# Transformer block on eight cores: first stage reordered with late projections as fillers, and three edits in the experts

## The chip, the cores and the metric

The kernel runs on the 8 cores of one Trainium2 chip. Every core computes one batch element of 2048 rows with the same program and exchanges nothing with the others. The metric is the device time of the slowest core in microseconds (us). Its matmul engine is called PE below, the vector engine DVE, the scalar engine ACT, GpSimd POOL; SP is the engine whose queue issues plain DMAs.

## The reference

For each batch element (2048 rows of 1024) a parallel block is computed: row normalisation, then causal attention with 16 heads of 64, and beside it a mixture of 4 experts, of which each row uses 2.

```python
xn = _layernorm(x, axis=-1)
x = x + _L0_attn_ref(xn, w_qkv, w_out) + _L0_ffn_ref(xn, w1, b1, w2, b2, wr, br)

# _L0_attn_ref: q, k, v of xn; softmax(q k^T / 8, causal) v; then w_out
# _L0_ffn_ref:
logits = xf @ wr + br
topk_vals, topk_idx = jax.lax.top_k(logits, K)            # K = 2 of E = 4
gates = jax.nn.softmax(topk_vals, axis=-1)
h = jax.nn.gelu(jnp.einsum('nd,edh->enh', xf, w1) + b1[:, None, :], approximate=False)
y = jnp.einsum('enh,ehd->end', h, w2) + b2[:, None, :]
c = jnp.einsum('eh,ehd->ed', jax.nn.gelu(b1, approximate=False), w2) + b2
c_sum = c.sum(axis=0)
out = jnp.einsum('nk,nkd->nd', gates, y_sel - c_sel + c_sum[None, None, :])
```

The constants c of the four experts give every row an additional sum: a "constant row" that depends on its gates alone. The hidden size is 4096.

## The kernel before

Work is emitted engine by engine in program order. `W(engine, semaphore, value)` (L234) makes an engine wait, `I` (L238) emits an instruction that raises a semaphore, `E` (L246) one that does not. Each engine and each DMA-issuing queue runs its list in order.

**First stage (L254 to L529).** SP loads the rows of x in eight blocks of 256 rows (`xt`, L255), with the biases b1, the router weights wr (one partition, 16 KB) and br between the first and second block. PE then spreads wr to all partitions in eight pieces (L336) and ACT copies them out (L339). A loop over j (L503) handles two tiles of 128 rows each time: `norm_stats(j)` (DVE L442 to L453, ACT L455 and L457, POOL L461), `transpose_out` of the tiles of the turn before (DVE L497 for the even tile, ACT L499 for the odd), `norm_rows` (ACT L469 writes the normalised rows `xnb`, of which there are four buffers, and SP stores them to `xn_tm`, L475, one store waiting for the one before), V projections (`v_group`, 8 matmuls, evicted by ACT in this stage), Q and K projections of head pair 0 (`qk_group`, evicted by DVE L389), `transpose_in` (PE L483), and some halves of the router's logits (`logit`, DVE L428). From the fifth tile on, `norm_rows` waits for the store that last used its buffer: `W("scalar", "SXN", 16 * (ts - 3))`.

**Attention (L532 to L1037).** A head pair takes 40 steps (query tile qt of 512, key tile kb of 128): two score matmuls (L568), an exponential on ACT (L585), a causal mask on DVE (L591), two matmuls with V (L607). At the last kb of a qt DVE copies the result (L621). Between them `fill` pops single matmuls from a list of groups of 8, `pair_fill` (L941), spread over the pair by the planner's `cost` (L951). Pair hp holds the 8 Q/K groups of pair hp+1, and for hp below 4 also four V groups of heads 8 to 15. Without V groups a pair has 64 filler matmuls, with them 96. `load_wqk(hp + 2)` (L270) is issued by POOL at the start of a pair. `dveq` hands out the rest of the logits and the routing to DVE.

**Experts (L1049 to L1379).** An expert has two steps, u = 0 and 1, each over half of the hidden size. `emit_h` (L1085) makes 16 chunks hc of h (L1101, ACT GELU L1112), `emit_y` (L1244) multiplies tile by tile with w2 (32 matmuls, L1281), DVE scales into `yacc` (L1297, L1300), and in step u = 1 POOL adds each tile to y by an indirect DMA (`scatter`, L1065). Weights come by POOL's queue, four loads of w1 (L914) and four of w2 (L922) for each step. Steps are numbered 0 to 7. Depending on how many rows an expert gets on a core, a step has nine tiles (one of 64 rows) or eight. Two extra jobs run inside. The constants: `g_rows` (L1134) multiplies GELU(b1) with w2; for the last expert its w2 is loaded in eight pieces to `gw` by `load_gw` (L1205), the first at the start of `emit_y` of step 0, and read at tile 4 and at the last tile of steps 0 to 3. The constant rows: `dense` (L1223) makes one tile of 128 rows in PE (L1231), DVE copies it to one of four buffers (L1236) after the DMA that used that buffer has landed (`SCD`), and POOL adds it to y (L1241). All 16 run in step 6: eight in `emit_h`, after each odd hc, eight in `emit_y`, one before each of the tiles 0 to 7.

## Time and profile before

| | us |
|---|---|
| median of 3 runs | 1701.55 |
| lowest and highest run | 1693.19, 1892.82 |
| the profiled execution | 1698.15 |
| its slowest core, first to last instruction (the span) | 1696.6 |
| spans of the other seven cores | 1675.2 to 1692.7 |
| PE busy on the slowest core | 1508.3 (89%) |
| ACT, DVE, POOL busy | 637.6, 486.7, 215.2 |

All rows are of core 7, the slowest, unless they name another. The span begins with the first instruction of the core; 1.55 us of the profiled execution lie around it. A bracket at the end of a row of the timeline holds how long the engine had been idle and what ended it. "PEclk" is the share of the full TensorE clock that was granted.

### The profile page before, as it was taken

The page shows a single profiled execution, that of the slowest core. Times are in us where ns is not written, and L with a number is a line of the kernel's source. Part 1 is how long each engine was busy: PE and PEld are TensorE (multiplying, and loading weights), DVE is VectorE, ACT ScalarE, POOL GpSimd, SP SyncE. Part 2 cuts the span into 40 slices and gives each one's busy share as a digit, 9 for nine tenths or more (in the row PEclk, how much of TensorE's full clock was granted, in tenths as well). Part 3 has the DMA queues.
Part 4 walks back from the last instruction along what each step waited for, and adds up shares of the span by engine and source line. Part 5 has one row for each costly group of instructions (what it writes and reads, how often), then busy time and mean ns, then how long its engine had stood idle before and what let it go on. Part 6 is the DMA issues. An engine that isn't in the chain of part 4 may idle for free.

```text
span 1696.6 us, 22095 instructions; the slowest of 8 cores (1675.2 to 1696.6 us)
## 1 busy us (share of the span) xinstructions
PE 1508.3 (89%) x7616; PEld 664.6 (39%) x7616; DVE 486.7 (29%) x879; ACT 637.6 (38%) x809; POOL 215.2 (13%) x233
## 2 busy tenths in 40 slices
PE   4778889877888889989997999998999999978996
PEld 2333223222322235534643444443434445534642
DVE  3675665677333321122022012011011022122011
ACT  3448788766789762300400310400401402300410
POOL 2001211000001000102013002112020022111012
PEclk9989999988999799989999999999999999999998
DMA  8140000030004667685978934997942987894424
GB/s 249 63 75 1 13 14 1 13 50 14 13 15 99 137 139 176 155 127 114 153 120 133 142 50 88 170 140 107 143 93 34 141 132 114 126 143 76 87 40 75
DMA packets 113627, 160.14 MB, mean 94 GB/s; under 512 B 41813, under 2 KB 74709, under 8 KB 113113
## 3 DMA queue, kind: packets, MB, share of 16 engines
q0 software_dynamic: 66096, 119.55, 45.7%
q1 hardware_dynamic: 47402, 38.91, 8.8%
q8 instruction: 77, 1.26, 0.3%
q14 instruction: 52, 0.43, 0.1%
HBM read 194.09 MB, written 38.80 MB: 137 GB/s over the span
## 4 chain that ended last, share of the span: by engine, by line
PE 74%; ACT 7%; DVE 6%; DMA 6%; issue 5%; DVEq 1%; ACTq 0%; POOL 0%; SPq 0%; POOLq 0%; another core or an unknown queue 0%
PE P L1101 27%; PE P L1281 24%; PE P L382 5%; PE P L607 5%; ACT p L585 4%; PE P L568 4%; DMA y<-dst 2%; PE P L1179 2%; DMA gw<-w 2%; PE P L398 2%; DVE usb L621 2%; PE P L892 1%; PE P L1162 1%; ACT rcp L629 1%; ACT rcp L628 1%
## 5 line engine op out<-in xcount | busy, mean ns | idle before, releaser
L1101 PE MATMUL P<-xg,w1b 128*128 128x363 bf16 (+2 forms) x2560 | 468.8, 345 | 18.2 <-issue 15.7
L1281 PE MATMUL P<-w2b,h_sb 128*128 128x512 bf16 (+1 forms) x2176 | 467.4, 383 | 17.7 <-DVE yacc L1297 9.8
L1112 ACT ACTIVATE h_sb<-P,b_sb 128x363 bf16<-128x363 f32 (+1 forms) x320 | 195.2, 613 | 587.5 <-PE P L1101 505.6
L585 ACT ACTIVATE p<-P,cneg,c 128x1024 bf16<-128x1024 f32 (+1 forms) x320 | 330.0, 1072 | 76.4 <-PE P L568 67.3
L1101 PEld LDWEIGHTS P<-xg,w1b 128*128 128x128 bf16 x2560 | 251.3, 98 | 236.4 <-issue 31.1
L1281 PEld LDWEIGHTS P<-w2b,h_sb 128*128 128x128 bf16 (+1 forms) x2176 | 207.1, 99 | 279.0 <-issue 42.7
L607 PE MATMUL P<-p,v_sb 128*128 128x512 bf16 (+3 forms) x640 | 180.2, 362 | 20.4 <-DVE p L591 13.1
L382 PE MATMUL P<-xn_fm,wp 128*128 128x512 bf16 x512 | 150.1, 393 | 12.8 <-ACT v_sb L409 6.3
L568 PE MATMUL P<-q,k 64*128 64x512 bf16 (+3 forms) x640 | 119.1, 368 | 44.6 <-ACT p L585 43.8
L1300 DVE SCALAR_TENSOR_TENSOR yacc<-P,gate_sb,yacc 128x1024 f32<-128x1024 f32 x32 | 41.1, 1284 | 407.1 <-PE P L1281 401.5
L1297 DVE TENSOR_SCALAR yacc<-P,gate_sb 128x1024 f32<-128x1024 f32 x32 | 41.1, 1284 | 329.8 <-PE P L1281 323.3
L428 DVE SCALAR_TENSOR_TENSOR junk<-xt,mv,wr_bc 128x512 bf16<-128x512 f32 x128 | 101.6, 812 | 5.5
L568 PEld LDWEIGHTS P<-q,k 64*128 64x128 bf16 x640 | 32.5, 93 | 168.1 <-issue 167.1
L607 PEld LDWEIGHTS P<-p,v_sb 128*128 128x128 bf16 x640 | 57.4, 99 | 94.8 <-issue 48.3
L1112 ACT ACT_TABLE_LOAD x4 | 5.1, 1283 | 214.2 <-PE P L1101 214.2
L1081 POOL DMA_INDIRECT y<-yacc,idx_sb x32 | 50.4, 1576 | 248.6 <-DVE yacc L1300 167.0
L398 PE MATMUL P<-wv,xn_fm 128*128 128x512 bf16 x256 | 71.6, 406 | 1.6 <-DVE xn_fm L497 1.6
L914 POOL DMA_DIRECT2D w1b<-w x32 | 28.6, 922 | 344.3 <-PE P L1101 266.6
L382 PEld LDWEIGHTS P<-xn_fm,wp 128*128 128x128 bf16 x512 | 41.4, 98 | 77.1 <-issue 53.2
L591 DVE TENSOR_TENSOR p<-p,tri_bf 128x256 bf16<-128x256 bf16 x128 | 38.2, 303 | 98.6 <-ACT p L585 97.6
L639 POOL TENSOR_TENSOR cat<-usb,rcp 64x512 bf16<-64x512 f32 x24 | 32.5, 1352 | 106.9 <-ACT rcp L631 106.0
L621 DVE COPY usb<-P 128x512 f32<-128x512 f32 x64 | 41.2, 685 | 16.6 <-PE P L607 16.3
(163 smaller groups left out, 694.2 us busy)
## 6 DMA issues: line engine op xcount, KB each, us to landing
w1b<-w POOLq DMA_DIRECT2D x32, 1024.0 KB, 16.1
w2b<-w POOLq DMA_DIRECT2D x32, 1024.0 KB, 18.4
xt<-x SPq DMA_DIRECT2D x8, 1024.0 KB, 19.0
xr<-x SPq DMA_DIRECT2D x16, 512.0 KB, 4.3
y<-xr SPq DMA_DIRECT2D x16, 512.0 KB, 5.0
gw<-w POOLq DMA_DIRECT2D x8, 1024.0 KB
y<-dst POOLq DMA_DIRECT2D x16, 512.0 KB, 11.2
wp<-wqk POOLq DMA_DIRECT2D x8, 512.0 KB, 6.0
```

The lines of the kernel that those rows point to most:

```text
L382: mms = [lambda t, bank, dc=dc: t.matmul(bank, w[:, dc * 256 + o:dc * 256 + o + 128], xn_fm[:, dc * S + tt * 512:dc * S + (tt + 1) * 512], ...
L398: mms = [lambda t, bank, dc=dc: t.matmul(bank, xn_fm[:, dc * S + ts * 128:dc * S + (ts + 1) * 128], wv[half][:, dc * 512:(dc + 1) * 512], ...
L428: E("vector", lambda v: v.scalar_tensor_tensor(junk[:, half * 512:(half + 1) * 512], xtile(ts)[:, half * 512:(half + 1) * 512], mv[:, 2 * ...
L568: fn = (lambda t, h=h: t.matmul(sb[:, h * 512:h * 512 + n], k_sb[hp % 2][h * 64:h * 64 + 64, kb * 128:(kb + 1) * 128], q_sb[hp % 2][h * 64 ...
L585: v_exp[i] = I("scalar", "SS", lambda s: s.activation(dst, src, AF.Exp, bias=cneg8[:, 0:1], scale=c0125[:, 0:1]))
L607: fn = (lambda t, h=h: t.matmul(P45[:, h * 512 + qo:(h + 1) * 512], v_sb[:, o + h * 64:o + h * 64 + 128], p[:, h * 512:h * 512 + n], start ...
L621: last_u[h] = ("SV", I("vector", "SV", lambda v, h=h: v.tensor_copy(u[:, h * 512:(h + 1) * 512], P45[:, h * 512:(h + 1) * 512])))
L1081: I("gpsimd", "SA%d" % (t % 2), lambda g: g.indirect_dma_start(y_h.ap(), bass.IndirectOffsetOnAxis(idx_sb[:, q:q + 1], 0), yacc[:, t * 102 ...
L1101: fn = (lambda t, b=b, hc=hc, dc=dc, o=o, n=n, bank=bank: t.matmul(bank[:, 0:n], w1b[b][:, dc * 512 + (hc % 4) * 128:dc * 512 + (hc % 4 + ...
L1112: geluv[i] = I("scalar", "SS", lambda s, hc=hc, o=o, n=n, bank=bank, col=col: s.activation(h_sb[:, hc * PITCH + o:hc * PITCH + o + n], ban ...
L1281: fn = (lambda tt, b=b, k=k, off=off, rows=rows, r=r, half=half, pt=pt: tt.matmul(pt[r:r + rows, half * 512:(half + 1) * 512], h_sb[:, k * ...
L1297: evict[i] = I("vector", "SV", lambda v, t=t, gate=gate, pt=pt: v.tensor_scalar_mul(yacc[:, t * 1024:(t + 1) * 1024], pt[:], gate))
```

## The change

It has these parts:

- The router weights come as one DMA that writes all 128 partitions (2 MB), last of SP's first loads; the spreading by PE and ACT goes. The eight loads of x stand back to back. The bias columns and GELU(b1) are made later (end of the first stage, start of the experts).
- In the loop of the first stage the statistics of block j+1 come ahead of the logits and the projections of turn j. The loop has nine turns; logits begin in turn 3 with 6, then 7, 7, 7, 7, 6. The V groups of tiles 12 to 15 and the Q/K groups of query tiles 2 and 3 of pair 0 leave it.
- Those eight groups become fillers of pair 0 (16 groups, 128 matmuls). The V groups of the other heads move to pairs 1, 2 and 3 (5, 5 and 6 instead of 4 in each of pairs 0 to 3). The load of wqk for pair 2 comes at qt = 3 of pair 0. A fourth place for `usb` is used in the first half of pair 0, since the old one still holds V weights.
- In the experts, the first `load_gw` is issued after chunk 13 of `emit_h` of step 0, behind the last w2 load of that step and ahead of the last waits for step 1's w1.
- `dense` runs three times in `emit_h` of step 6 (chunks 5, 9, 13), eight times in `emit_y` of step 6, and five times in `emit_h` of step 7.
- The last tile of step 7 is computed in two halves of 512 columns; each is scaled and added to y by a DMA of its own.

```diff
@@ -182,7 +183,7 @@
     p_sb = [at(f"p{i}", [128, 1024], BF16, o_p + 2048 * i) for i in range(3)]
     rcp = at("rcp", [128, 512], F32, o_p + 6144)
 
-    usb = [at(f"usb{i}", [128, 1024], F32, o) for i, o in enumerate((o_wv, o_p + 16384, o_qk))]
+    usb = [at(f"usb{i}", [128, 1024], F32, o) for i, o in enumerate((o_wv, o_p + 16384, o_qk, o_qk + 12288))]
     coefT = at("coefT", [128, S], BF16, o_p + 20480)
     cat = at("cat", [128, NPAIR * S], BF16, o_cat)
     wv = [at(f"wv{i}", [128, 4096], BF16, o_wv + 8192 * i) for i in range(2)]
@@ -255,14 +256,13 @@
         I("sync", f"SXD{j}", lambda e, j=j: e.dma_start(
             xt[2 * j][:].rearrange("p (t d) -> p t d", d=1024),
             x_h.ap()[j * 256:(j + 1) * 256, :].rearrange("(t p) d -> p t d", p=128)), 16)
-        if j == 0:
-            v_b1 = I("sync", "SX", lambda e: e.dma_start(
-                b1st[:].rearrange("r (k c) -> r k c", k=4),
-                b1_h.ap().rearrange("k (r c) -> r k c", r=32)), 16)
-            v_wr = I("sync", "SX", lambda e: e.dma_start(
-                wr_bc[0:1, :], wr_h.ap().rearrange("(a k) d -> a (k d)", a=1)), 16)
-            v_br = I("sync", "SWR", lambda e: e.dma_start(
-                br_bc[:], bass.AP(br_h, 0, [[0, 128], [1, 4]])), 16)
+    v_b1 = I("sync", "SX", lambda e: e.dma_start(
+        b1st[:].rearrange("r (k c) -> r k c", k=4),
+        b1_h.ap().rearrange("k (r c) -> r k c", r=32)), 16)
+    v_br = I("sync", "SWR", lambda e: e.dma_start(
+        br_bc[:], bass.AP(br_h, 0, [[0, 128], [1, 4]])), 16)
+    v_wr = I("sync", "SWRB", lambda e: e.dma_start(
+        wr_bc[:], bass.AP(wr_h, 0, [[0, 128], [1, 4096]])), 16)
 
     v_wq = {}
 
@@ -317,31 +317,17 @@
 
     W("scalar", "SG", v_c1)
     W("tensor", "SG", v_c1)
-    W("tensor", "SX", v_b1)
...
-    W("tensor", "SX", v_wr)
-    v_wb = {}
-    for c in range(8):
-        bank = (P45, P67)[c // 2 % 2][:, c % 2 * 512:(c % 2 + 1) * 512]
-        if c == 0:
-            W("tensor", "SS", v_b1c)
-        if c >= 4:
-            W("tensor", "SS", v_wb[c - 4])
-        v_t = I("tensor", "ST", lambda t, c=c, bank=bank: t.matmul(
-            bank, onesq[0:1, :], wr_bc[0:1, c * 512:(c + 1) * 512], start=True, stop=True))
+
+    def bias_columns():
+        W("tensor", "SX", v_b1)
+        v_t = 0
+        for e_ in range(NE):
+            v_t = I("tensor", "ST", lambda t, e_=e_: t.transpose(
+                P45[0:128, e_ * 32:(e_ + 1) * 32], b1st[0:32, e_ * 128:(e_ + 1) * 128], ident[0:32, 0:32]))
         W("scalar", "ST", v_t)
-        v_wb[c] = I("scalar", "SS", lambda s, c=c, bank=bank: s.activation(
-            wr_bc[:, c * 512:(c + 1) * 512], bank, AF.Identity))
-    W("scalar", "SS", v_b1c)
-    v_hf = I("scalar", "SS", lambda s: s.activation(hfake[:], b1_sb[:], AF.Gelu))
-
-    guard = [("SS", v_wb[6]), ("SS", v_wb[7])]
+        return I("scalar", "SS", lambda s: s.activation(b1_sb[:], P45[:, 0:128], AF.Identity))
+
+    guard = [("SS", 0), ("SS", 0)]
     bank_i = [0]
     trg = [("ST", 0), ("ST", 0)]
     xn_ev = {}
@@ -386,6 +372,8 @@
 
         def evict(bank, v):
             W("vector", "ST", v)
+            if hp == 1 and tt == 0:
+                W("vector", *u_read[0])
             e = I("vector", "SV", lambda d: d.tensor_copy(dst[:, tt * 512:(tt + 1) * 512], bank))
             (q_ev if isq else k_ev)[(hp, tt)] = ("SV", e)
             return ("SV", e)
@@ -500,10 +488,9 @@
         trg[ts % 2] = xn_ev[ts]
 
     first_logits = [(ts, k, half) for ts in (0, 1, 2, 3, 8) for k in range(NE) for half in range(2)]
-    for j in range(10):
-        if j < 8:
-            v_nm = norm_stats(j)
-        if 1 <= j <= 8:
+    v_nm = norm_stats(0)
+    for j in range(9):
+        if j >= 1:
             transpose_out(2 * j - 2)
             transpose_out(2 * j - 1)
         if j < 8:
@@ -511,29 +498,33 @@
             norm_rows(2 * j + 1, v_nm)
             if j == 6:
                 load_wqk(1)
-        if j >= 2:
+        if j < 7:
+            v_nm = norm_stats(j + 1)
+        for _ in range((0, 0, 0, 6, 7, 7, 7, 7, 6)[j]):
+            logit(*first_logits.pop(0))
+        if 2 <= j < 8:
             for ts in (2 * j - 4, 2 * j - 3):
                 run_all(v_group(0, ts, True))
-            if j % 2 == 1:
+            if j % 2 == 1 and j < 7:
                 run_all(qk_group(0, (j - 3) // 2, False))
                 run_all(qk_group(0, (j - 3) // 2, True))
         if j < 8:
             transpose_in(2 * j)
             transpose_in(2 * j + 1)
-        for _ in range((0, 0, 4, 5, 5, 5, 5, 5, 5, 6)[j]):
-            logit(*first_logits.pop(0))
         if j == 5:
             E("vector", lambda v: v.drain())
             v_t01 = I("vector", "SV", lambda v: v.memset(cnt[:, 0:1], 0.0))
             W("gpsimd", "SV", v_t01)
             load_wv(1)
 
+    v_b1c = bias_columns()
+
 
     steps = [(hp, qt, kb) for hp in range(NPAIR) for qt in range(4) for kb in range(4 * qt + 4)]
     n_st = len(steps)
     v_qk, v_exp, v_msk, v_av = {}, {}, {}, {}
     v_mult = {}
-    last_u = [("SV", C["SV"])] * 2
+    last_u = [("SS", v_b1c)] * 2
     u_read = [("SG", C["SG"])]
     pend, later = [], []
     W("scalar", "SV", C["SV"])
@@ -943,9 +940,15 @@
         a = []
         for tt in range(4):
             a += [qk_group(hp + 1, tt, False), qk_group(hp + 1, tt, True)]
-        if hp < 4:
-            vs = [v_group(1, ts, False) for ts in range(4 * hp, 4 * hp + 4)]
-            a = [x for pr in zip(a[0::2], a[1::2], vs) for x in pr]
+        if 1 <= hp <= 3:
+            vs = [v_group(1, ts, False) for ts in ((), range(0, 5), range(5, 10), range(10, 16))[hp]]
+            a = [x for q in range(4) for x in a[2 * q:2 * q + 2] + vs[q:q + 1]] + vs[4:]
+        if hp == 0:
+            late = []
+            for ts in range(12, 16):
+                late.append(v_group(0, ts, False))
+            a = [qk_group(0, 2, False), qk_group(0, 2, True)] + late + \
+                [qk_group(0, 3, False), qk_group(0, 3, True)] + a
         pair_fill[hp] = [(x, 8) for x in a]
 
     def cost(i):
@@ -967,12 +970,13 @@
             tot = sum(u for _, u in pair_fill[hp])
             cum, csum_ = 0.0, sum(cost(k) for k in range(i, i + 40))
             popped[0] = 0
-            if hp < NPAIR - 2:
-
-                W("gpsimd", "ST", C["ST"])
-                load_wqk(hp + 2)
             if hp == NPAIR - 1:
                 W("gpsimd", "ST", C["ST"])
+        if hp < NPAIR - 2 and kb == 0 and qt == (0 if hp else 3):
+
+            assert ("k", hp, 3) in done and ("q", hp, 3) in done
+            W("gpsimd", "ST", C["ST"])
+            load_wqk(hp + 2)
         if hp == 4 and qt == 0 and kb == 3:
             W("gpsimd", "ST", C["ST"])
             W("gpsimd", *u_read[0])
@@ -1039,6 +1043,8 @@
         W("tensor", *g_)
 
 
+    DENSE = [(6, hc) for hc in (5, 9, 13)] + [(7, hc) for hc in (1, 4, 7, 10, 13)]
+
     PH = [P45[:, 0:512], P45[:, 512:1024], P67[:, 0:512], P67[:, 512:1024]]
     PY = [P01, P23]
 
@@ -1084,6 +1090,8 @@
 
         def emit_h(step, cols):
             e_, u = divmod(step, 2)
+            if first and step == 0:
+                E("scalar", lambda s: s.activation(hfake[:], b1_sb[:], AF.Gelu))
             if u == 0:
                 W("tensor", "SXT", xgv[e_])
             for hc in range(16):
@@ -1115,7 +1123,7 @@
                     gel[(step, hc)] = geluv[i]
                 if hc % 4 == 3:
                     hblk[(step, b)] = v_g
-                if first and step == 6 and hc % 2 and state["ts"] < NTS:
+                if first and (step, hc) in DENSE:
                     dense()
                 if first and step == 0 and o_late:
                     o_tile(o_late.pop(0))
@@ -1123,6 +1131,8 @@
                     W("gpsimd", "ST", v_g)
                     W("gpsimd", *u_read[0])
                     emit_w2(0, hc // 4)
+                    if hc == 13:
+                        load_gw()
 
         def py_next():
             i = state["y"]
...
@@ -1241,13 +1251,37 @@
             I("gpsimd", f"SCD{ts % 4}", lambda g: g.dma_start(
                 y_h.ap()[ts * 128:(ts + 1) * 128, :], dst4[ts % 4][:], accum_op=ALU.add), 16)
 
+        def last_tile(t):
+
+            i, pt = py_next()
+            q = tile_q(NE - 1, t)
+            for half in range(2):
+                c = slice(half * 512, (half + 1) * 512)
+                v_y = 0
+                for hc in range(16):
+                    fn = (lambda tt, hc=hc, c=c: tt.matmul(
+                        pt[:, c], h_sb[:, hc * PITCH + t * 128:hc * PITCH + t * 128 + 128],
+                        w2b[hc // 4][:, (hc % 4) * 1024 + c.start:(hc % 4) * 1024 + c.stop],
+                        start=(hc == 0), stop=(hc == 15)))
+                    if hc == 15:
+                        v_y = I("tensor", "ST", fn)
+                    else:
+                        E("tensor", fn)
+                W("vector", "ST", v_y)
+                yc = yacc[:, t * 1024 + half * 512:t * 1024 + (half + 1) * 512]
+                evict[i] = I("vector", "SV", lambda v, c=c, yc=yc: v.scalar_tensor_tensor(
+                    yc, pt[:, c], gate_sb[:, q:q + 1], yc, ALU.mult, ALU.add))
+                W("gpsimd", "SV", evict[i])
+                I("gpsimd", f"SAL{half}", lambda g, half=half, yc=yc: g.indirect_dma_start(
+                    y_h.ap().rearrange("s (h c) -> (s h) c", h=2),
+                    bass.IndirectOffsetOnAxis(idx2[:, half:half + 1], 0), yc, None, compute_op=ALU.add), 16)
+
         def emit_y(step, tiles):
             e_, u = divmod(step, 2)
             v_ga = 0
             last = len(tiles) - 1
             if first and step == 0:
                 c_init()
-                load_gw()
             for p, (off, rows) in enumerate(tiles):
                 t = off // 128
                 if first and step < 6 and p == 1:
@@ -1262,8 +1296,11 @@
                     load_gw()
                 if first and step < 6 and p == 2:
                     g_sum(e_, v_ga)
-                if first and step == 6 and state["ts"] < NTS:
+                if first and step == 6 and p < 8:
                     dense()
+                if first and step == 7 and p == last:
+                    last_tile(t)
+                    break
                 i, pt = py_next()
                 v_y = 0
                 for hc in range(16):
```

## Rows read from the trace of the kernel before

**Rows 1.** Cores, the slowest: span and mean granted clock
```profile
core 7: 1696.6 us, clock 0.961
```

**Rows 2.** Chain of work that ended last, in order of time: start us, us, what
```profile
15.54 14.00 PE P L336 x16
```

**Rows 3.** L255 at 18 to 19 us, the last load of x: duration ns, start; landing
```profile
L255 SPq DMA_DIRECT2D xt<-x x1: 3027/3027/3027, 18.4 to 18.4; - x1
DMA to landing us min/median/max: 21.6/21.6/21.6
```

**Rows 4.** L475 at 34 to 34.5 us, the first store of normalised rows
```profile
L475 SPq DMA_DIRECT2D xn_tm<-xnb x1: 345/345/345, 34.2 to 34.2; - x1
DMA to landing us min/median/max: 6.5/6.5/6.5
```

**Rows 5.** Page, DMA issues: out<-in, engine, count, KB each, median us to landing
```profile
xn_tm<-xnb SPq DMA_DIRECT2D x16, 256.0 KB, 2.2
```

**Rows 6.** Windows: span, length, PE, PEld, DVE, ACT, POOL busy, PEclk, DMA share, GB/s
```profile
24.00:27.00 3.00, 3.00 (x5) 1.23 (x4) 1.15 (x5) 1.19 (x2) 0.00 (x0) 1.00 1.00 328
```

**Rows 7.** Timeline of DVE, a turn of the first stage: start us, us, what
```profile
55.84 0.69 DVE L389 CAST q<-P 128x512 bf16<-128x512 f32 x1 [1.04 <-PE P L382]
56.62 0.75 DVE L428 SCALAR_TENSOR_TENSOR junk<-xt,mv,wr_bc 128x512 bf16<-128x512 f32 x1
...
60.32 2.47 DVE L442 BATCH_NORM_STATS2 bst<-xt 128x6 f32<-128x512 f32 x4
...
63.34 1.23 DVE L497 CAST xn_fm<-P 128x1024 bf16<-128x1024 f32 x1
```

**Rows 8.** Timeline of ACT: rows 4 and 5 normalised, and the first exponential
```profile
42.08 2.36 ACT L469 ACTIVATE xnb<-xt,nmr_a,r_a 128x1024 bf16<-128x1024 f32 x2
...
117.94 2.75 ACT L585 ACTIVATE p<-P,cneg,c 128x1024 bf16<-128x1024 f32 x3 [3.76 <-DVE q L389]
```

**Rows 9.** Timeline of DVE: the copy at the end of pairs 1, 2, 5 and 6
```profile
240.15 1.28 DVE L621 COPY usb<-P 128x512 f32<-128x512 f32 x2
...
300.76 1.28 DVE L621 COPY usb<-P 128x512 f32<-128x512 f32 x2
...
501.24 1.28 DVE L621 COPY usb<-P 128x512 f32<-128x512 f32 x2
...
555.49 1.28 DVE L621 COPY usb<-P 128x512 f32<-128x512 f32 x2
```

**Rows 10.** Timeline of PE: tile 4 of step 0, and of step 1
```profile
757.01 1.04 PE L1140 MATMUL P<-gw,hfake 128*32 128x512 bf16 x8 [8.06 <-DMA gw<-w]
757.98 26.18 PE L1281 MATMUL P<-w2b,h_sb 128*64 128x512 bf16 x128
...
886.50 0.61 PE L1140 MATMUL P<-gw,hfake 128*32 128x512 bf16 x8
888.11 24.47 PE L1281 MATMUL P<-w2b,h_sb 128*64 128x512 bf16 x128 [0.99 <-DVE yacc L1300]
```

**Rows 11.** Timeline of POOL: DMA issues at the ends of h of steps 0 and 6
```profile
718.92 0.77 POOL L1211 DMA_DIRECT2D gw<-w  x1
...
1481.83 3.84 POOL L914 DMA_DIRECT2D w1b<-w  x4
```

**Rows 12.** Timeline of PE in step 6, emit_y: tile 0, constant row ahead of tile 5, tile 5
```profile
1480.98 7.07 PE L1281 MATMUL P<-w2b,h_sb 128*128 128x512 bf16 x32 [1.33 <-DVE dst L1236]
...
1529.05 1.01 PE L1231 MATMUL P<-cst,coefT 96*128 96x512 bf16 x2 [9.86 <-DVE dst L1236]
1530.13 8.42 PE L1281 MATMUL P<-w2b,h_sb 128*128 128x512 bf16 x32
```

**Rows 13.** Chain of work that ended last, in order of time
```profile
1485.36 42.12 DMA y<-dst
...
1680.91 1.29 DVE yacc L1300
```

**Rows 14.** Windows at the end of the span, same columns as rows 6
```profile
1686.00:1688.00 2.00, 0.00 (x0) 0.00 (x0) 0.00 (x0) 0.00 (x0) 0.00 (x0) 0.50 0.98 186
```

More of the change, by code:

```diff
@@ L156, in build_nc @@
     gateh = small("gateh", [128, 4])
+    idx2 = small("idx2", [128, 2], I32)
     unf = small("unf", [128, 64])
@@ L422, in logit @@
         if (ts, k, half) == (0, 0, 0):
-            W("vector", "SS", v_wb[7])
+            W("vector", "SWRB", v_wr)
             W("vector", "SWR", C["SWR"])
@@ L616, in emit_av @@
         if sp:
-            u = usb[0 if hp < 4 else 1 if hp < NPAIR - 1 else 2]
+            u = usb[3 if hp == 0 and qt < 2 else 0 if hp < 4 else 1 if hp < NPAIR - 1 else 2]
             W("vector", "ST", v_av[i])
@@ L838, in evict @@
                 gate_sb[:, e_ * 16:(e_ + 1) * 16], cmpa[:, 96:112], cmpa[:, 64:80], ALU.add))
+            if e_ == NE - 1:
+                for half in range(2):
+                    VD(lambda d, half=half: d.tensor_scalar(
+                        cmpa[:, 112 + half:113 + half], cmpa[:, 87:88], 2.0, float(half), ALU.mult, ALU.add))
+                E("vector", lambda d: d.tensor_copy(idx2[:], cmpa[:, 112:114]))
             for r in (0, 64):
@@ L1242, in dense @@
                 y_h.ap()[ts * 128:(ts + 1) * 128, :], dst4[ts % 4][:], accum_op=ALU.add), 16)
+        def last_tile(t):
+            i, pt = py_next()
+            q = tile_q(NE - 1, t)
+            for half in range(2):
+                c = slice(half * 512, (half + 1) * 512)
[17 more added lines that the diff above has]
+                    bass.IndirectOffsetOnAxis(idx2[:, half:half + 1], 0), yc, None, compute_op=ALU.add), 16)
         def emit_y(step, tiles):
@@ L1375, in ffn @@
                 expert(e_, *EVEN)
-        W("gpsimd", "SA0", C["SA0"])
-        W("gpsimd", "SA1", C["SA1"])
+        for k in ("SA0", "SA1", "SAL0", "SAL1"):
+            W("gpsimd", k, C[k])
     ffn(0, PITCH // 128, True)
```

10 lines of the change are left out of this document (2 added, 8 removed).

## Prediction, made before the changed kernel was run

> **What bounds the kernel now.** I read the page first: PE is busy 89% of the span, so time can be won only where PE stands still, runs at half clock, or at the end. The view of the cores gives the time that counts, core 7 with 1696.6 us [rows 1]; the profiled execution took 1698.15 us, 1.55 us around the span. Then I followed the chain of waits and the timelines stage by stage.
>
> *First stage, to 117.94 us.* PE spends 14 us spreading the router weights [rows 2], and ACT, which copies them out, normalises nothing meanwhile. But that is not all that holds the stage. The last block of x is issued at 18.4 us and lands 21.6 us later, at 40.0 [rows 3]. The first store of normalised rows, issued at 34.2, lands at 40.7 [rows 4], 6.5 us later where the usual store takes 2.2 [rows 5]: SP's transfers land in their order. The fifth tile, which needs that store's buffer, is normalised at 42.08 [rows 8]. After that the stage is a ring: DVE computes five logits in 60.32 - 56.62 = 3.70 us and only then the statistics of the next block, 3.02 us [rows 7]; ACT waits for these, PE for ACT, and DVE for PE's projections. The first exponential starts at 117.94 [rows 8].
>
> *Attention.* Pair 6, with 64 fillers, takes 555.49 - 501.24 = 54.25 us from the end of pair 5 to its own; pair 2, with 96, takes 300.76 - 240.15 = 60.61 [rows 9]. A filler costs (60.61 - 54.25)/32 = 0.20 us: PE is nearly the bound, and there is little idle time for more.
>
> *Experts.* PE runs almost without a gap. One gap is the first wait for `gw` [rows 10], another the constant row before tile 5 of step 6, which waits for a DMA of 42.12 us [rows 12, 13].
>
> **The change part by part.**
>
> *Opening.* PE's 14 us and ACT's copies go. This alone doesn't start the fifth tile earlier: its buffer still waits for the first store, and that store now stands behind x and behind 2 MB of router weights. Loads ran at 328 GB/s with the DMA engines full [rows 6]: 2 MB take 6.4 us. The x blocks end at 40.0 as before (the engines are full from early on, with x and POOL's weights; the order of x changes, not the sum), the router weights at 46.4, the store 0.7 later, at 47.1. The fifth tile starts 5.0 us later than before, not earlier.
>
> The Trainium skill (DMA: Bandwidth & Descriptors, Bandwidth) times one load of 1 MB at 6.15 us, which would make 12.3 us of the 2 MB and 1680 of the sum below; the trace, with loads in a queue, has 6.4 in rows 6.
>
> *The turns.* From the fifth tile to the end of the next evicted q took 55.84 + 0.69 - 42.08 = 14.4 us before [rows 7, 8]. The opening turn 3 has the same members, so 61.5. From there the statistics are early, PE and ACT have less than DVE, and DVE sets the pace. A turn costs it 1.2 (copy) + 3.0 (statistics) + 7 x 0.74 = 9.4 us. Turns 4, 5 and 6: 28.2, with two evictions of 0.69 in turn 5 29.6; turn 7 without statistics 6.4; the copy in turn 8 1.2. Sum 37.2, so 98.7; with the first scores (estimated at 0.8 with their hand-overs) the first exponential starts at 99.5. That is 18.4 us earlier. Six logits still stand on DVE before the first mask, as before, so that costs nothing new. The bias columns (four small transposes, one copy) lie on PE and ACT in those turns, where both wait for DVE; without that cover about 1 us. GELU(b1) moves to ACT ahead of its first chunk, where PE is the slower; nothing.
>
> *The fillers.* Eight groups of 8 matmuls leave the stage, 64 fillers come into attention (32 more in pair 0; 8, 8 and 16 in pairs 1 to 3). At 0.20 each +12.7 us. Lower bound 8, if a third falls into waits for exponentials; upper 64 x 7.07/32 = 14.1, the full price of a matmul [rows 12]. Their eight evictions (0.69 each) go to DVE in pair 0, which has room while PE is the bound. The load of wqk for pair 2 goes one whole query tile ahead of its use: nothing. POOL waits there for PE's latest matmul; behind it stand only normalisations of `cat`, needed in the last pair.
>
> *gw.* With the wait, tile 4 of step 0 costs 8.06 + 1.04 + 26.18 = 35.3 us; the same stretch in step 1, 0.61 + 0.99 + 24.47 = 26.1 [rows 10]. The difference, 9.2, includes matmuls at the lower clock behind the gap. `gw` was issued at 718.92, behind four w1 loads [rows 11]. Now it is issued just behind the last w2 load, some 7 us earlier and with 4 MB fewer ahead; it lands well before 749. The w1 loads that it overtakes land when `gw` did before (757 at the latest) and are needed only at the next step, near 785. -9.2. Bound: -7, if something else is late there.
>
> *Constant rows.* The number of matmuls is the same. At the border of h and y two constant rows no longer collide: -1.3 [rows 12]. The gap before tile 5: 9.86, less the ordinary 0.99, plus 0.40 and 1.35 for slow matmuls behind it [rows 10, 12], 10.6 us. What was late is the DMA of the constant row of tile 0, queued behind four w1 loads that began at 1481.83 [rows 11], landing 45.7 us after them [rows 13]. The row that waits now still uses a buffer four rows back, and that is again tile 0's. But POOL reaches the w1 loads after chunk 13 and not after chunk 15. Two chunks are some 7.4 us of PE (2 x 24 matmuls of 363 columns at the rate of rows 12); less the hand-over, the queue is 5.6 us ahead of PE compared with before. The gap shrinks by 5.6, and I add 0.9, half of what the lower clock cost: -6.5. Bounds 0 and -10.6. The five rows in step 7's h add what they took from step 6; their DMAs are done in its 59 us before the first scatter.
>
> *Last tile.* PE ends at the same time. DVE's 1.29 [rows 13] halves, and of the last transfer (2 us at 98% [rows 14]) half is already gone: -0.6 - 1.0 = -1.6. Bounds 0 (POOL issues one more DMA) and -2.3.
>
> **Sum.** -18.4 + 12.7 - 9.2 - 6.5 - 1.3 - 1.6 = -24.3; 1698.15 - 24.3 = **1673.9 us**. The median of the runs shown is 3.4 above the profiled execution; the forecast goes by the latter.
>
> **The rivals.**
>
> *A. The stores do not queue behind the loads.* Then the fifth tile is early and turn 3 waits only for the router weights: 46.4 + 6 x 0.74 + 1.4 = 52.2 in place of 61.5, 9.3 less: 1664.6. Against it: rows 3 and 4, the store landing 0.7 behind x. Chance 0.15. The Trainium skill (DMA: Bandwidth & Descriptors, Queues, rings and completion order) says that descriptors are consumed in ring order and yet that completion isn't strictly first-in first-out; in rows 4 it was in order.
>
> *B. Attention hides half of the fillers.* ACT is busy most of that stage, and PE waits for it in places. Then 6.4 instead of 12.7: 1667.6. Against it rows 9. Chance 0.10.
>
> *C. The constant rows' edit does not do what it says:* the same buffer waits for the same DMA behind the same four loads, and the gap stays. 1680.4. For it: the pairing is unchanged. Against it: the loads start earlier relative to PE. Chance 0.12.
>
> *D. Slower: the router weights' DMA.* It reads the same 16 KB 128 times, which no row shows. Each us it takes over 6.4 delays the fifth tile and all behind it. It outweighs the other gains from 30.7 us on (68 GB/s); at 50 GB/s it takes 42 us and the time is 1709. For it: only that it is new and in front of all stores. Against it: its 16 KB rows are longer than those of x. Chance 0.05; slower by over 2% (1736) would need 95 us, 0.02.
>
> **How the numbers follow.** The likeliest case (0.58) is the sum, 1662 to 1685. Best bounds together: -27.7 + 8 - 9.2 - 10.6 - 1.3 - 2.3 = -43.1, 1655; worst, with router weights at half the rate: -12.0 + 14.1 - 7 - 1.3 = -6.2, 1692. The range is 1656 to 1690. Two per cent, about what a measurement of this kernel can tell from no change, is 34 us: faster begins at 1667.5. Faster: A, half of B and a sixth of the likeliest, 0.30. Slower 0.02. Same 0.68.
>
> **What would show it.** First exponential near 99.5 and the fifth tile near 47 (near 30: rival A). Pair 0 some 6.5 us longer. No wait of `g_rows` for `gw` in step 0. A wait of about 4 us for a constant row in step 6 on core 7; on cores where that wait was absent no gain from it. The prediction is wrong if the first stage is paced by PE or ACT, if the router weights land after 50, or if a new wait appears in pair 0 for q, k or V.

## The result, and the profile of the changed kernel

| | before, us | after, us |
|---|---|---|
| median | 1699.44 | 1675.43 |
| lowest run | 1693.19 | 1670.97 |
| the profiled execution | 1698.15 | 1675.64 |
| its slowest core (7) | 1696.6 | 1674.1 |
| the other seven cores | 1675.2 to 1692.7 | 1654.8 to 1671.6 |

The changed kernel takes 0.987 of the time of before, 95% interval 0.9827 to 0.9913: 22.5 us less on core 7, a gain that is clear of noise but within 2%. The forecast for the profiled execution was 1673.9, and it took 1675.64. The table's medians are of all runs, one of them disturbed (1892.82 us, before); every ratio, and every median in the experiments, is of undisturbed runs alone, by which the kernel before has 1697.33.

The page of the changed kernel, then the places that answer to the rows of before. First ACT's timeline at the fifth tile and at the first exponential [rows 8]:

```profile
span 1674.1 us, 22048 instructions; the slowest of 8 cores (1654.8 to 1674.1 us)
...
47.16 1.24 ACT L457 ACTIVATE xnb<-xt,nmr_a,r_a 128x1024 bf16<-128x1024 f32 x1 [13.99 <-DMA xn_tm<-xnb]
...
102.47 2.75 ACT L576 ACTIVATE p<-P,cneg,c 128x1024 bf16<-128x1024 f32 x3 [4.90 <-PE P L559]
```

The fifth tile starts at 47.16, not at 42.08: earlier statistics and a free PE brought it nothing, since ACT had been idle for 13.99 us until the first store landed. On the other cores it starts at 46.6 to 49.3. The views of three of SP's DMAs say why, the last block of x, the load of the router weights and the first store behind it (the last two numbers of an issue's row are its first and last start):

```profile
L256 SPq DMA_DIRECT2D xt<-x x1: 6344/6344/6344, 12.8 to 12.8; - x1
DMA to landing us min/median/max: 27.4/27.4/27.4
...
L264 SPq DMA_DIRECT2D wr_bc<-wrt x1: 1444/1444/1444, 25.3 to 25.3; - x1
DMA to landing us min/median/max: 21.1/21.1/21.1
...
L463 SPq DMA_DIRECT2D xn_tm<-xnb x1: 1729/1729/1729, 26.9 to 26.9; - x1
DMA to landing us min/median/max: 20.2/20.2/20.2
```

The last block of x lands at 12.8 + 27.4 = 40.2, the weights at 25.3 + 21.1 = 46.4, 6.2 us behind it, the store at 47.1, 0.7 later, though it had been issued 20.2 us before. This is the order of [rows 3, 4] with 2 MB more in it.

Then PE and DVE in turn 5, the one turn of 4 to 7 that did not run as reckoned, and PE's first scores (the second row). The last two rows are windows: length, busy time of PE, PEld, DVE, ACT and POOL with instructions, granted clock, DMA share, GB/s:

```profile
76.81 6.54 PE L368 MATMUL P<-xn_fm,wp 128*128 128x512 bf16 x16 [6.25 <-ACT v_sb L397]
...
101.76 0.93 PE L559 MATMUL P<-q,k 64*128 64x512 bf16 x4 [5.05 <-DVE xn_fm L485]
...
80.49 0.69 DVE L377 CAST k<-P 128x512 bf16<-128x512 f32 x1 [0.18 <-PE P L368]
83.46 0.69 DVE L377 CAST q<-P 128x512 bf16<-128x512 f32 x1 [2.27 <-PE P L368]
...
71.00:77.00 6.00, 0.19 (x1) 0.14 (x2) 5.76 (x13) 1.56 (x4) 0.19 (x1) 0.91 0.11 44
77.00:83.40 6.40, 6.40 (x20) 2.40 (x19) 3.86 (x11) 0.00 (x0) 0.00 (x0) 0.55 0.01 3
```

PE, with nearly nothing to do from 71 to 77, got 0.55 of its clock just behind that: sixteen matmuls took 6.54 us, where sixteen of the same shape take 3.61 in this stage at a granted 1.00 (experiment 3). DVE, which paces the stage, waited 2.27 us for them.

Attention, DVE's copies at the ends of pair 0 and of pair 7 [rows 9]:

```profile
169.58 1.28 DVE L612 COPY usb<-P 128x512 f32<-128x512 f32 x2
...
613.35 1.29 DVE L612 COPY usb<-P 128x512 f32<-128x512 f32 x2 [0.70 <-PE P L598]
```

The last copy was at 616.96 before. Of the 15.5 us won up to the first exponential, 3.6 are left here. The mean of the eight cores says much the same: the first exponential moved from 119.0 to 102.5, the last copy from 616.3 to 611.3.

The experts. PE at tile 4 of step 0 [rows 10], POOL's issues there [rows 11], then PE before tile 5 of step 6 [rows 12], POOL's issues at its start, and the link of the chain that held the constant row ([rows 13]; columns start, us, what):

```profile
745.62 0.61 PE L1150 MATMUL P<-gw,hfake 128*32 128x512 bf16 x8
747.23 24.47 PE L1318 MATMUL P<-w2b,h_sb 128*64 128x512 bf16 x128 [1.00 <-DVE yacc L1334]
...
708.10 0.75 POOL L1221 DMA_DIRECT2D gw<-w  x1
708.83 2.65 POOL L911 DMA_DIRECT2D w1b<-w  x3
...
1505.79 0.72 PE L1241 MATMUL P<-cst,coefT 96*128 96x512 bf16 x2 [2.03 <-DVE dst L1246]
1506.87 8.37 PE L1318 MATMUL P<-w2b,h_sb 128*128 128x512 bf16 x32 [0.36 <-DVE yacc L1334]
...
1460.34 2.97 POOL L911 DMA_DIRECT2D w1b<-w  x3
1465.99 0.88 POOL L911 DMA_DIRECT2D w1b<-w  x1 [2.68 <-PE P L1241]
1467.69 0.92 POOL L1251 DMA_DIRECT2D y<-dst  x1 [0.83 <-DVE dst L1246]
...
1467.69 36.52 DMA y<-dst
```

The wait of 8.06 for `gw` is gone and nothing else took its place. The wait of 9.86 is 2.03. The loads of w1 behind the third constant row begin at 1460.34, 7.4 us ahead of the y DMA of tile 0's constant row; before, at 1481.83, the first of them stood 3.5 us ahead of it.

Last, a stall that grew (PE at the start of step 2's h):

```profile
921.78 4.31 PE L1109 MATMUL P<-xg,w1b 128*128 128x512 bf16 x10 [11.12 <-issue]
927.82 2.54 PE L1109 MATMUL P<-xg,w1b 128*128 128x512 bf16 x11 [1.72 <-issue]
```

The whole on core 7, forecast against the two traces:

| term | forecast | measured |
|---|---|---|
| first exponential | 117.94 to 99.5: -18.4 | to 102.47: -15.5 |
| 64 fillers in attention | +12.7 | 499.02 to 510.88: +11.9 |
| attention's end to the start of step 0's `emit_y` | 0 | 100.33 to 100.65: +0.3 |
| `gw`: `emit_y` of step 0 to h of step 1 | -9.2 | 77.22 to 68.05: -9.2 |
| constant rows: `emit_y` of step 6 to h of step 7 | -6.5 | 81.53 to 73.65: -7.9 |
| border of h and y | -1.3 | -1.3 |
| last tile: PE's end to the end of the span | -1.6 | 15.8 to 14.4: -1.4 |
| all else | 0 | +0.5 |
| span | -24.3 | -22.5 |

"All else" is what the stretches named leave of the span; the stall of step 2 is in it. The terms are rounded one by one.

### The profile page after: what moved, and what is told of

Same layout as the page of the kernel before. It is cut to its first block, busy times and chain, and to the rows that moved or that the text cites. A ratio compares the mean times of both kernels' runs of the same rounds, so it can differ in the third digit from the quotient of the medians.

```text
span 1674.1 us, 22048 instructions; the slowest of 8 cores (1654.8 to 1674.1 us)
## 1 busy us (share of the span) xinstructions
PE 1492.8 (89%) x7600; PEld 659.5 (39%) x7600; DVE 487.7 (29%) x887; ACT 630.5 (38%) x796; POOL 215.5 (13%) x234
## 4 chain that ended last, share of the span: by engine, by line
PE 72%; DVE 6%; issue 6%; ACT 5%; another core or an unknown queue 4%; DMA 4%; DVEq 1%; POOL 1%; ACTq 0%; POOLq 0%; SPq 0%
PE P L1109 28%; PE P L1318 22%; PE P L368 6%; PE P L598 5%; PE P L559 4%; ACT p L576 3%; PE P L1189 2%; DMA y<-dst 2%; PE P L386 2%; DVE usb L612 2%; DVE junk L416 1%; DMA xn_tm<-xnb 1%; PE P L889 1%; PE P L1172 1%
## 5 line engine op out<-in xcount | busy, mean ns | idle before, releaser
L1318 PE MATMUL P<-w2b,h_sb 128*128 128x512 bf16 (+1 forms) x2144 | 457.3, 380 | 17.3 <-DVE yacc L1334 11.1
L1318 PEld LDWEIGHTS P<-w2b,h_sb 128*128 128x128 bf16 (+1 forms) x2144 | 203.3, 99 | 271.5 <-issue 37.3
L368 PE MATMUL P<-xn_fm,wp 128*128 128x512 bf16 x512 | 154.1, 408 | 12.7 <-ACT v_sb L397 6.2
L368 PEld LDWEIGHTS P<-xn_fm,wp 128*128 128x128 bf16 x512 | 42.3, 101 | 81.4 <-issue 59.6
L1246 DVE COPY dst<-P 128x1024 f32<-128x1024 f32 x16 | 19.5, 1222 | 106.2 <-PE P L1241 101.8
L471 PE MATMUL P<-identb,xnb 128*128 128x128 bf16 x128 | 11.4, 252 | 42.4 <-ACT xnb L457 40.5
## 6 DMA issues: line engine op xcount, KB each, us to landing
w1b<-w POOLq DMA_DIRECT2D x32, 1024.0 KB, 16.8
```

The source lines that it names most:

```text
L368: mms = [lambda t, bank, dc=dc: t.matmul(bank, w[:, dc * 256 + o:dc * 256 + o + 128], xn_fm[:, dc * S + tt * 512:dc * S + (tt + 1) * 512], ...
L1318: fn = (lambda tt, b=b, k=k, off=off, rows=rows, r=r, half=half, pt=pt: tt.matmul(pt[r:r + rows, half * 512:(half + 1) * 512], h_sb[:, k * ...
```

## The experiments

Each kernel computes the whole reference. Times in the text are of core 7 where no other is named. The kernel before ran on each of the chips too; medians are compared within one chip only, unless the text says otherwise. One core of one profile is a thin basis: in two profiles of one kernel the first exponential of core 7 differs by up to 3.2 us. So where it matters the mean of the eight cores stands beside core 7.

**1. The old spreading in the new order.** One partition of router weights (16 KB) is loaded behind the first block of x, and PE and ACT spread it as before; all else is the changed kernel.

```diff
+        if j == 0:
+            v_wr = I("sync", "SWRB", lambda e: e.dma_start(
+                wr_bc[0:1, :], wr_h.ap().rearrange("(a k) d -> a (k d)", a=1)), 16)
...
-    v_wr = I("sync", "SWRB", lambda e: e.dma_start(
-        wr_bc[:], bass.AP(wr_h, 0, [[0, 128], [1, 4096]])), 16)
...
+        v_t = I("tensor", "ST", lambda t, c=c, bank=bank: t.matmul(
+            bank, onesq[0:1, :], wr_bc[0:1, c * 512:(c + 1) * 512], start=True, stop=True))
```

> The changed kernel, but the router weights come again as 16 KB to one partition (behind the first block of x) and are spread by PE and ACT ahead of the loop. If the opening is set by the first store standing behind 2 MB of router weights, the fifth tile is normalised at 41 to 42 us in place of 47.2, although PE and ACT spend some 14 us more in the opening, and the first exponential moves from 102.5 to 96 to 98; the whole gets about 5 us faster (1670). The rival (the store does not queue; ACT's and PE's copies are what matters): the first rows come later, at 25 to 30 us, and the first exponential comes at 102 or later, 0 to 8 us slower.

Measured (the second row is PE in turn 5):

```profile
43.10 1.24 ACT L470 ACTIVATE xnb<-xt,nmr_a,r_a 128x1024 bf16<-128x1024 f32 x1 [8.33 <-DMA xn_tm<-xnb]
...
75.02 6.18 PE L381 MATMUL P<-xn_fm,wp 128*128 128x512 bf16 x16 [6.22 <-ACT v_sb L410]
```

The last block of x in this run:

```profile
L256 SPq DMA_DIRECT2D xt<-x x1: 6692/6692/6692, 16.0 to 16.0; - x1
DMA to landing us min/median/max: 26.1/26.1/26.1
```

The fifth tile is 4.1 us earlier than with the DMA, and again waits for the first store. With the 2 MB gone the store's landing moved by 4 us, not by the 6.2 they took: it lands at 43.0, 0.9 behind the last block of x, which in this run lands at 16.0 + 26.1 = 42.1 and not at 40.2. The first exponential of core 7 is at 100.32, only 2.2 earlier than 102.47: the eighth tile waits for a store once more (at 52.37), and turn 5's Q/K group runs at the lower clock again. Core 7 gained least, though. On the mean of the eight cores the fifth tile is at 42.3 and the first exponential at 98.1, 4.4 earlier than in the changed kernel and about as expected. Attention's last copy is 7.0 earlier, on core 7 (606.37) as on the mean (604.3); where the rest of that comes from is not shown. Median 1670.83 us, 0.982 of the kernel before, interval 0.9756 to 0.9884; this overlaps the changed kernel's, so by the time of the whole the difference is not shown.

So the DMA that took 14 us from PE did not shorten the stage; it lengthened it by 2.2 us on core 7 and by 4.4 on the mean. The gain of the first stage came from the rest of the change: 12.5 of the 15.5 us from the eight groups that left it (experiment 6), the remainder from the new order.

**2. The router weights loaded twice**, to price the queue.

```diff
+    v_wr = I("sync", "SWRB", lambda e: e.dma_start(
+        wr_bc[:], bass.AP(wr_h, 0, [[0, 128], [1, 4096]])), 16)
```

> The changed kernel with the 2 MB load of the router weights issued twice, one after the other has landed, both ahead of the first store on SP's queue. The theory: the fifth tile moves by 6.4 us plus the fixed time of one more transfer, so from 47.2 to 54 to 56, and the first exponential by the same amount, to 109 to 111; the whole 7 to 9 us slower. The rival (DVE's logits pace the stage and the opening has slack): the first exponential moves by less than 3 us.

```profile
59.47 1.24 ACT L459 ACTIVATE xnb<-xt,nmr_a,r_a 128x1024 bf16<-128x1024 f32 x1 [24.85 <-DMA xn_tm<-xnb]
```

The fifth tile is 12.3 us later, the first exponential at 114.23, 11.8 later, attention's last copy at 621.57, 8.2 later; one run, 1689.34 us. On the mean of the eight cores the fifth tile is 9.5 later and the first exponential 9.4. That the fifth tile's time passes to the first exponential nearly one for one is confirmed. The size was missed on core 7: both loads raise the same semaphore, so the second was issued only when the first had landed, at 49.1, and took 9.6 us alone; on core 0, the slowest of that run, it was issued at 47.1 and took 7.7. In the queue behind x the same 2 MB cost 46.4 - 40.2 = 6.2. The Trainium skill (DMA: Bandwidth & Descriptors, Bandwidth) has 6.15 us for one load of 1 MB, from which the prediction worked out 12.3 for 2 MB. The same row gives 341 GB/s, and by that rate, an estimate, 2 MB take 6.1 us: the trace agrees with the rate and not with the time for 1 MB.

**3. Logits earlier**, on top of experiment 1: DVE is idle while it waits for stores, and the router weights are there by then.

```diff
-        for _ in range((0, 0, 0, 6, 7, 7, 7, 7, 6)[j]):
+        for _ in range((0, 0, 12, 4, 4, 5, 5, 5, 5)[j]):
```

> As e6_old_spread, and the 40 first logits are dealt out as 12 in turn 2 and 4, 4, 5, 5, 5, 5 in turns 3 to 8 (6, 7, 7, 7, 7, 6 in the changed kernel from turn 3). The router weights are there by then, and DVE stands still for 14.5 us before the fifth tile. The theory (DVE paces the turns): turns 4 to 7 lose 3, 2, 2 and 2 logits of 0.74, 6.7 us, so the first exponential comes at 90 to 93, some 5 to 7 earlier than in e6_old_spread, as far as PE and ACT keep up; the whole near 1664. The rival (PE at half clock and its waits for ACT's evictions already pace the turns): less than 3 us earlier than e6_old_spread.

```profile
94.34 2.75 ACT L589 ACTIVATE p<-P,cneg,c 128x1024 bf16<-128x1024 f32 x3 [3.37 <-PE P L572]
...
65.67 3.61 PE L399 MATMUL P<-wv,xn_fm 128*128 128x512 bf16 x16 [1.02 <-ACT v_sb L410]
73.16 5.30 PE L381 MATMUL P<-xn_fm,wp 128*128 128x512 bf16 x16 [3.87 <-ACT v_sb L410]
```

On core 7 the first exponential is at 94.34, 6.0 us before experiment 1's and 1.3 us later than my bound. The other cores do not bear this out. On the mean of the eight it is at 96.6 (93.1 to 99.0), 1.4 before experiment 1's, and the last copy is 1.6 earlier (602.7); the repetition below gives 1.9 and 0.7. That is the rival's less than 3 us. With fewer logits DVE is done sooner, and PE at the lower clock is what it waits for: on core 4, and on core 7 in the repetition, the Q/K group of turn 3 took 5.30 as well. Two runs took 1668.48 and 1670.39 us; core 4, the slowest in the latter, waited 5.1 us for `gw`.

One core shows what the clock costs. All eight have the same 3.87 us of idle time ahead of turn 5's Q/K group. On seven the group takes 5.30 to 6.42 us. On core 2, whose granted clock was 1.00 throughout from 60 to 85 us, it takes 3.61:

```profile
73.33 3.61 PE L381 MATMUL P<-xn_fm,wp 128*128 128x512 bf16 x16 [3.87 <-ACT v_sb L410]
...
93.05 2.76 ACT L589 ACTIVATE p<-P,cneg,c 128x1024 bf16<-128x1024 f32 x3 [3.58 <-PE P L572]
```

From the start of that group to the first exponential it is 19.7 us on core 2, 21.2 on core 7 (5.30) and 21.9 to 22.3 on the six others (6.06 to 6.42): what the group loses by the clock passes on nearly whole. Why core 2 kept its clock is open.

**4. and 5. The same kernel and the changed one side by side on one chip**, with no edit beyond the above.

> The same kernel as e9_early_logits (router weights spread by PE and ACT, 12 logits in turn 2). In its profile attention ended at 600.4 us on core 7 against 613.4 in the changed kernel. If that carries through to the end, it is 8 to 13 us faster than e11_changed_again (1662 to 1667) on the same chip; the rival (a later wait for DMAs takes it back on some core) gives less than 5 us.

> The changed kernel itself, beside e12_early_logits_again on one chip. Near 1675 us, 1.4% below the kernel before.

The changed kernel: first exponential 102.49, median 1673.3, ratio 0.9843 (0.9793 to 0.9892). With old spreading and early logits: 97.49, last copy at 603.42 against 609.72, median 1668.9, ratio 0.9816 (0.9769 to 0.9864). It is 4.4 us faster by the medians, below the 8 to 13 expected; the intervals overlap, so this is likely and not shown. Nearly all of it is experiment 1's part: the last copy is 6.9 us earlier than the changed kernel's on the mean of the eight cores, and the early logits account for 0.7 of that.

The repetition also shows how near luck lies to a forecast for one core. In it core 7 of the changed kernel took 1663.6 us instead of 1674.1, and cores 0 and 3 set the time with 1671.6 and 1671.7.

**6. The late projections back in the first stage**, the fillers of attention as before.

```diff
-        if 2 <= j < 8:
+        if j >= 2:
...
-            if j % 2 == 1 and j < 7:
+            if j % 2 == 1:
...
-        if 1 <= hp <= 3:
-            vs = [v_group(1, ts, False) for ts in ((), range(0, 5), range(5, 10), range(10, 16))[hp]]
...
+        if hp < 4:
+            vs = [v_group(1, ts, False) for ts in range(4 * hp, 4 * hp + 4)]
```

> The changed kernel with its eight late projection groups (V of tiles 12 to 15, Q/K of query tiles 2 and 3 of pair 0) put back into the first stage, at the ends of turns 7 to 9; pair_fill as before. The theory (the turns are paced by DVE, PE has room in turns 7 and 8): the first exponential moves from 102.5 to about 111 or 112 us (two more evictions in turn 7, then V of tiles 14 and 15, one Q/K pair and its evictions behind the last copy), and attention gets 64 fillers back at 0.19 each, 11.9 us. Net 1 to 4 us faster than the changed kernel, with the last copy of attention near 610. The rival (the projections cost their full PE time in the stage, 14 us, and fillers are partly hidden): the first exponential at 116 or later and 2 us slower or more.

```profile
114.97 1.20 ACT L576 ACTIVATE p<-P,cneg,c 128x1024 bf16<-128x1024 f32 x1 [0.27 <-PE P L559]
...
176.53 1.28 DVE L612 COPY usb<-P 128x512 f32<-128x512 f32 x2
```

The first exponential comes 12.5 us later (11.0 if the fifth tile's 1.5 is taken off, 48.63 against 47.16), pair 0 takes 61.56 instead of 67.11, and attention from the first exponential on 9.3 us less: 501.6 against 510.9. The last copy is at 616.58, 3.2 us later. I had expected it earlier. The error is in the first half: I had reckoned that the stage would hide most of the groups, and it hid little: 11.0 of the 64 x 7.07/32 = 14.1 us that their matmuls take at full clock. Late projections as fillers are worth 11.0 - 9.3 = 1.7 to 12.5 - 9.3 = 3.2 us on core 7 and 12.1 - 10.3 = 1.8 on the mean of the eight cores, by one profile (1685.52 us).

**7. The three edits of the experts alone**, on the kernel before: `load_gw` after chunk 13, the new `DENSE` list, the split last tile.

> The kernel before with the three edits in the experts alone (gw, constant rows, last tile). The theory adds the parts: 9.2 for gw, 7.9 and 1.3 for the constant rows, 1.3 at the end, together 18 to 20 us less than before on core 7 (near 1679). The first stage would then be worth 3 to 5 us. The rival (the parts do not add, since earlier stages shift DMAs of the eight cores against one another): 12 us or less, or 24 and more.

Median 1681.1 against 1698.57 on that chip, ratio 0.9893 (0.9869 to 0.9917): -17.5, where the sum of my four terms was -18.6. On core 7 nothing waits for `gw`, and the row before tile 5 waits 4.26 us. Core 1, the slowest, waits 7.9 us for a later piece of `gw`, at the last tile of step 1. First exponential at 120.89, last copy at 620.07. On the mean of the eight cores the last copy is at 617.1, and at 611.3 in the changed kernel: 5.8 us is what first stage and fillers are worth together at that point, where -18.4 + 12.7 = -5.7 had been forecast. The whole times come from different chips, and their intervals overlap.

**8. `gw` back** at the start of `emit_y` of step 0.

```diff
-                    if hc == 13:
-                        load_gw()
...
                 c_init()
+                load_gw()
```

> The changed kernel with the first load of gw issued again at the start of emit_y of step 0, behind the four w1 loads. The theory: PE waits again about 8 us for gw before tile 4 of step 0 and runs slower behind it, so the stretch from the start of emit_y of step 0 to the start of h of step 1 grows from 68.05 to about 77.2 us, and the whole by 9. The rival (the wait only moved elsewhere, to w1 or w2 of the next steps): the stretch grows, but the whole changes by less than 4 us.

```profile
753.16 1.05 PE L1148 MATMUL P<-gw,hfake 128*32 128x512 bf16 x8 [7.67 <-DMA gw<-w]
```

The wait is back on all eight cores, 4.9 to 10.2 us. From the start of `emit_y` to h of step 1 it takes 76.1 us instead of 68.05, +8.1. Median 1687.97, ratio 0.9939 (0.9918 to 0.996), against 0.987 and 0.9843 for the changed kernel on other chips; the medians are 12 to 15 us apart.

**9. The constant rows back:** eight in step 6's h, eight in its y.

```diff
-                if first and (step, hc) in DENSE:
+                if first and step == 6 and hc % 2 and state["ts"] < NTS:
...
-                if first and step == 6 and p < 8:
+                if first and step == 6 and state["ts"] < NTS:
```

> The changed kernel with the sixteen constant rows dealt out as before (eight in h and eight in y of step 6). The theory: on core 7 (and core 0) the wait ahead of tile 5 comes back, 8 to 10 us; on cores that did not have it in the trace of before (1, 3) only 1.3 us at the border. The slowest core gets 8 to 11 us slower. The rival (the wait on core 7 came from the alignment of cores in that run and is not tied to the order): no wait over 3 us and about 2 us slower.

```profile
1510.54 1.01 PE L1241 MATMUL P<-cst,coefT 96*128 96x512 bf16 x2 [6.24 <-DVE dst L1246]
```

That is core 7; core 1 waits 10.54, core 0 2.4, cores 3 to 5 not at all, while I had named core 0 and excluded core 1. The border's 1.33 is back, and core 7's stretch from `emit_y` of step 6 to h of step 7 takes 78.0 us instead of 73.65. Median 1688.44, ratio 0.9944 (0.9916 to 0.9972). The edit brings back the wait, but on which cores it falls changes from run to run: in the rerun of the changed kernel and in experiment 8 core 7 does not wait at all.

**10. Is it the place of the loads, or the smaller number of rows?** The third of the three rows in step 6's h goes from chunk 13 to chunk 15, so that POOL reaches the w1 loads two chunks later; the number of rows stays.

```diff
-    DENSE = [(6, hc) for hc in (5, 9, 13)] + [(7, hc) for hc in (1, 4, 7, 10, 13)]
+    DENSE = [(6, hc) for hc in (5, 9, 15)] + [(7, hc) for hc in (1, 4, 7, 10, 13)]
```

> The changed kernel, but the third constant row of h in step 6 is made after chunk 15 instead of 13; the number in each part stays. The theory (the wait depends on when POOL reaches the w1 loads, which stand behind that row's DMA): the w1 loads begin some 8 us later against PE, and on core 7 the wait for a constant row's buffer ahead of tile 5 goes from 2.0 back to 8 to 10 us, with 1.3 at the border; the slowest core 7 to 11 us slower. The rival (fewer constant rows' DMAs in h made the gain): the wait stays under 4 us and the whole within 3 us.

```profile
1510.58 1.01 PE L1241 MATMUL P<-cst,coefT 96*128 96x512 bf16 x2 [9.23 <-DVE dst L1246]
...
1463.84 3.84 POOL L911 DMA_DIRECT2D w1b<-w  x4
```

The loads begin 3.5 us ahead of the row's DMA instead of 7.4, the wait is 9.23 instead of 2.03, the stretch 80.65 instead of 73.65. The slowest core of this profile takes 1683.6, 9.5 over the changed kernel's. So the gap shrank by the place of the loads and not by the number of rows.

All profiles together say the same without leaning on core 7. Where the loads begin 3.5 us ahead of the row's DMA (the kernel before, experiments 9 and 10), a row waits over 0.5 us on 10 of 24 cores, on six of them over 6 us, 10.54 at most. Where they begin 6.9 to 7.4 us ahead (the ten other profiles), one waits on 12 of 80 cores, on one of them over 5 us (6.26).

**11. The last tile whole.**

```diff
-                if first and step == 7 and p == last:
-                    last_tile(t)
-                    break
```

> The changed kernel with the last tile of step 7 computed and added to y in one piece. The theory: from PE's last matmul to the end of the span it takes 15.8 us as before the change, where the changed kernel takes 14.5 (its last transfer moves half the bytes, DVE scales half). The rival (the third indirect DMA costs POOL what the halves save): no difference over 0.3 us.

One run, 1690.28 us, set by core 5, which waits 16.5 us for the last piece of `gw` at the last tile of step 3. From the end of the last matmul to the end of the span it is 15.9 to 16.8 us on the eight cores, 16.3 on the mean; in the changed kernel 14.2 to 14.9, 14.5 on the mean, and 14.6 in its repetition. So the halves are worth 1.7 to 1.8 us, with 1.4 on core 7 above.

## Why the prediction was right, and where not

- **The ring around the first store: right.** Fifth tile 47.16 against 47.1, weights at 46.4 as reckoned. To a tenth that is luck: on the other cores the tile is at 46.6 to 49.3, on core 7 of the repetition at 48.37. Rival A fell: the store did queue. The Trainium skill (DMA: Bandwidth & Descriptors, Queues, rings and completion order) says that a DMA's semaphore increments land only after every earlier write from the same DMA engine; the trace agrees, with a store that landed 20.2 us after its issue and 0.7 after the loads. The one on completion order that I cited for A did not show here. The trace cannot tell the two orders on that page apart, since consumption in ring order would place the store there too. Rival D fell too: 2 MB read from the same 16 KB took 6.2 us. (D's last figure was wrong by my own sum: 1736 is reached at 1736 - 1673.9 + 6.4 = 68.5 us, not at 95.)
- **DVE sets the pace: right, but one term was mis-sized.** The turns of DVE were forecast as 37.2 in sum from 61.5 on; they took 101.4 - 61.4 = 40.0. Turns 4 and 6 took 9.5 each, turn 7 6.3, for 9.4 and 6.4. Turn 5 took 13.4 for 10.8. The step that failed is "PE and ACT have less than DVE": true at full clock. I had counted PE's sixteen matmuls at 3.6 us, but in turn 5 ACT's evictions stand behind the statistics that DVE makes, PE waits for those evictions, and behind this gap of 6.25 us they took 6.54. The scores that end the stage had 0.8 in my sum and took 1.1 at the lower clock. These two (2.6 and 0.3) are the 3 us that the first exponential came late. On the six cores where that group stands in one row (all but 0 and 6) it took 5.0 to 6.5 us. That the clock is the cause, and costs the stage what it costs the group, core 2 of experiment 3 shows.
- **The fillers: right, at the low side.** 11.9 us on core 7, 11.5 on the mean of the eight cores and 10.9 in the repetition, for 12.7. Pair 0 grew by 5.5 (61.59 to 67.11) for 6.5. Experiment 6 gives 9.3 on core 7 and 10.3 on the mean. So a filler costs 0.15 to 0.19 us, and part of them does hide, between my price and rival B, which had half (6.4).
- **`gw`: right,** -9.17 for -9.2, and +8.1 when undone. The wait at tile 4 of step 0 stands on all cores of the kernel before (6.0 to 9.2 us) and of experiment 8, and on none of the 88 cores profiled with the new place. What I had not reckoned with are later pieces of `gw`: with the new place nine cores of seven profiles wait 4.2 to 16.5 us for one at the last tile of step 1 or 3, and in six of the seven that core set the time. The two profiles of the changed kernel have none of these waits, nor has the kernel before. Whether the new place has a part in them is open.
- **The constant rows: the mechanism was right, the size low.** The place of the w1 loads relative to the row's DMA decides how often and how long a row waits (experiments 9 and 10). I had kept 4 us of wait and found 2.03: -7.9 for -6.5. Rival C, that the gap stays, fell. That "cores where that wait was absent" gain nothing says little: which cores those are changes from run to run (experiment 9).
- **The last tile: right,** 1.4 to 1.8 for 1.6.
- **Not foreseen:** the start of step 2's h has a second stall of 1.72 us; its cause is open.
- **What I expected after the prediction and missed:** that leaving the late projections in the stage would be faster (experiment 6), that early logits would bring 5 to 7 us (experiment 3) and the whole 8 to 13 (experiment 4), and what a second load of the 2 MB costs (experiment 2).

The errors of the terms (+2.9, -0.8, -1.4, +0.2 and +0.9 elsewhere) come to +1.8 together; the sum is nearer than its parts, and that is luck.

## What to carry to other kernels

Before taking work from an engine, look at what the next instruction waits for last: here 14 us of PE work fell away and the stage's start moved back by 5 us, because the replacing DMA stood in the queue ahead of a store whose buffer was needed. The first store landed 0.7 us behind the last load issued on its queue before it, and 0.9 behind x in experiment 1. So look at what a new load is put in front of; behind the first stores, or on another queue, it might have cost nothing, which was not tried. A transfer that is waited for soon belongs ahead of bulk loads (`gw`, the constant rows). Where a wait falls on other cores from run to run, judge an edit by all cores. Where another engine sets the pace, reckon the matmuls behind each gap at both clock levels.

## What the runs showed of the hardware

- Between TensorE's two levels, 1.2 and 2.4 GHz, a paced stage keeps falling back: granted 0.91 over 6 us in which PE had 0.19 us of work, 0.55 over the 6.4 behind, 16 matmuls of 512 columns in 6.54 us (6.18, 5.30, 4.98 and 6.31 in four other runs) instead of 3.6. A gap of 3.87 us ahead was enough for 5.30 to 6.56 on 15 of the 16 cores that had it; on one the granted clock stayed at 1.00 and the group took 3.61. How to keep the clock there was not tried.
- A load that reads the same 16 KB for each of 128 partitions took 6.2 us for 2 MB in a queue behind x, about the rate of the loads of x before it (328 GB/s [rows 6] would make it 6.4), and 7.7 and 9.6 us alone (experiment 2, cores 0 and 7).
- A constant row's DMA of 0.5 MB, issued behind four weight loads of POOL's queue, lands 36.5 to 42.1 us later on core 7, and with the loads 3.5 us ahead of it instead of 7 PE waits for it on 10 of 24 cores instead of 12 of 80.
